# One program block for the attention of both batches, and weights cut ahead of the stage that uses them

## What is computed

```python
t = t + attn(ln(t))      # softmax(q k^T / 16) v over the 4096 tokens of a batch, float32
t = t + lstm(ln(t))      # gates from ln(t) @ U + b, and h @ V step by step over 4096 tokens
```

## Time and profile before

| | us |
|---|---|
| median of 3 runs | 3800.24 |
| lowest, highest | 3799.6, 3802.97 |
| the profiled execution, its time | 3802.11 |
| its span (first to last instruction) | 3800.3 |
| PE busy in it | 3490.2 (92%) |
| DVE, ACT, GpSimd busy | 2919.2, 2443.7, 1313.8 |

### The profile page before, as it was taken

The page is one execution under the profiler, slowest core; times in us unless marked ns, Lnnn a source line. Parts: engine busy times, 40 slices in busy tenths (PEclk is TensorE's granted clock), DMA queues, the critical chain, the costliest instruction groups (busy, mean ns, idle before and its releaser), DMA issues. The chain is left out here.

```text
span 3800.3 us, 81781 instructions
## 1 busy us (share of the span) xinstructions
PE 3490.2 (92%) x30707; PEld 2954.7 (78%) x30707; DVE 2919.2 (77%) x4367; ACT 2443.7 (64%) x6220; POOL 1313.8 (35%) x737
## 2 busy tenths in 40 slices
PE   8878888888889989999999989999999989899987
PEld 7755555555569978888888888888888878888886
DVE  4679999999968866777777766777777766777887
ACT  4548888888855555666666655666666633677775
POOL 0009999999955541000000011000000024222254
PEclk9979999999999989999999999999999989999999
DMA  5674111211124321000000010000000046555575
GB/s 147 197 205 112 44 40 44 61 44 39 44 72 139 114 92 45 18 18 18 18 18 18 18 45 12 18 18 18 18 18 12 12 161 213 167 142 143 146 227 164
DMA packets 198916, 294.19 MB, mean 77 GB/s; under 512 B 17744, under 2 KB 155088, under 8 KB 195536
## 3 DMA queue, kind: packets, MB, share of 16 engines
q1 hardware_dynamic: 189392, 281.88, 24.8%
q10 hardware_dynamic: 9216, 8.39, 0.6%
HBM read 197.67 MB, written 92.54 MB: 76 GB/s over the span
## 5 line engine op out<-in xcount | busy, mean ns | idle before, releaser
L741 POOL TENSOR_TENSOR mx_big<-mp_lvs,mx_big 128x1280 f32<-128x1280 f32 (+1 forms) x224 | 710.1, 3235 | 282.4 <-ACT mp_lvs L661 278.3
L716 DVE TENSOR_TENSOR mx_big<-mp_psL,mx_big 128x2816 f32<-128x2816 f32 (+1 forms) x224 | 691.0, 3142 | 20.7 <-PE mp_psO L606 18.0
L668 ACT ACTIVATE mp_cut<-mp_psO,mx_mask 128x128 f32<-128x128 f32 x2048 | 553.3, 405 | 139.1 <-PE mp_psO L606 109.3
L606 PE MATMUL mp_psO<-mx_big,mp_pair 128*16 128x256 f32 x8192 | 498.5, 383 | 110.0 <-DVE mx_big L716 82.1
L1597 PE MATMUL sv_psO<-at_v_hi,sv_p_hi 128*128 128x258 f32 x2048 | 583.9, 285 | 13.5 <-DVE sv_p_lo L1685 10.4
L1616 ACT ACTIVATE sv_S<-sv_psS,at_kb 128x512 f32<-128x512 f32 x512 | 353.0, 689 | 372.2 <-PE sv_psS L1571 300.2
L1597 PE MATMUL sv_psO<-at_v_lo,sv_p_hi 128*128 128x258 f32 x2048 | 578.7, 283 | 0.0
L1597 PE MATMUL sv_psO<-at_v_hi,sv_p_lo 128*128 128x258 f32 x2048 | 577.9, 282 | 0.0
L1660 DVE TENSOR_TENSOR sv_run<-sv_run,sv_S 128x512 f32<-128x512 f32 x448 | 313.7, 700 | 289.0 <-ACT sv_S L1616 289.0
L606 PEld LDWEIGHTS mp_psO<-mx_big,mp_pair 128*16 128x16 f32 x8192 | 327.6, 126 | 245.3 <-DVE mx_big L716 136.0
L1597 PEld LDWEIGHTS sv_psO<-at_v_hi,sv_p_hi 128*128 128x128 f32 x2048 | 386.3, 189 | 43.1 <-DVE sv_p_lo L1685 21.2
(11 more groups left out here) (301 smaller groups left out, 7723.0 us busy)
## 6 DMA issues: line engine op xcount, KB each, us to landing
re_xg<-xg SPq DMA_DIRECT2D x192, 384.0 KB, 3.3
xg<-ga_xg SPq DMA_DIRECT2D x32, 768.0 KB, 4.0
att<-mx_big SPq DMA_DIRECT2D x16, 1024.0 KB, 6.5
mp_pair<-att SPq DMA_DIRECT2D x128, 128.0 KB, 2.9
mx_big<-rv SPq DMA_DIRECT2D x14, 1024.0 KB, 11.7
fr_xr<-in_x SPq DMA_DIRECT2D x16, 512.0 KB, 4.7
fr_xl<-in_x SPq DMA_DIRECT2D x32, 256.0 KB, 4.2
rv<-fr_rvs SPq DMA_DIRECT2D x16, 512.0 KB, 3.2
```

The lines of the kernel that those rows point to most:

```text
L606: mm = pe.matmul(psO[32 * j:32 * j + 2 * H, c % 2, q, :], pair[:, s, :, :, c * YC + y], Z[:, c % 2, y, :], start=True, stop=True, tile_pos ...
L668: ins = nc.scalar.activation(cut[:, s, c, :, h * DK:(h + 1) * DK], psO[:, c % 2, :, h * DK:(h + 1) * DK], ACT.Copy, scale=mask[:, h:h + 1])
L716: nc.vector.tensor_tensor(Z[:, c % 2, 0:m], psL[:, s, 0:D].unsqueeze(1).broadcast_to([P, m, D]), rv_place(big, seventh, b, c)[:, 0:m], ALU ...
L741: nc.gpsimd.tensor_tensor(Z[:, c % 2, m:YC], lvs[:, s, :].unsqueeze(1).broadcast_to([P, YC - m, D]), rv_place(big, seventh, b, c)[:, m:YC] ...
```

## The change

The four blocks of attention become one. `attention` is split in `projections` and `weighing`, which return one function for each engine; `attention_block` calls them in turn in a single `nc.Block()`. Where a program block's end kept things apart, waits on semaphores now stand. The weights of batch 1 are cut by GpSimd in the last passes of weighing batch 0, its first token blocks are loaded there too, and GpSimd cuts U, the gates' weights, into the space of `k_hi` after the last score of batch 1. The gates' block loads and cuts no weights.

```diff
+def attention_block(nc):
+    with nc.Block() as block:
+        @block.sync
+        def _(sp):
+            clear_used(sp, PLAN["used"])
+            project0.sync(sp)
+            weigh0.sync(sp, project1)
+            project1.sync(sp)
+            weigh1.sync(sp, None)
...
-                clear_used(sp)          # at the end of each attention block
...
     class SecondKeyWeights:
-    def cut_hi(self, act): / def cut_lo(self, dve):
+    def cut(self, pool):
+        pool.wait_ge(self.shared.w_in, 32)
+        self.nc.gpsimd.tensor_copy(self.mt_hi[:, :, :], self.mt).then_inc(self.mt_hi_cut, 1)
+        pool.wait_ge(self.mt_hi_cut, 1)
+        self.nc.gpsimd.tensor_tensor(self.mt_lo[:, :, :], self.mt, self.mt_hi[:, :, :], ALU.subtract).then_inc(self.mt_cut, 1)
...
     projections, tensor:
+                if b > 0 and n == 0:
+                    pe.wait_ge(before.kept, before.units)
+                if b > 0 and n == 1:
+                    pe.wait_ge(before.shifted, before.units)
...
+                if b > 0 and n == 0:
+                    pe.wait_ge(before.evicted, before.evictions)
...
     weighing, sync, after the last loads of batch 0, then of batch 1:
+                    sp.wait_ge(p_kept, NU - R + 9)
+                    after.load_first(sp)                  # token blocks 1 and 2
+                if b > 0 and n == NBLK - 1:
+                    sp.wait_ge(q_cut, BLOCKS - 2)
+                    for j in range(3):
+                        if j == 2:
+                            sp.wait_ge(shared.u_cut, 1)
+                        sp.dma_start(q[:, j % 2, :]..., k_rows(PLAN["gates"][1][j])).then_inc(shared.u_in[j], 16)
...
     weighing, gpsimd:
+            if b == 0:
+                pool.wait_ge(p_kept, NU - R + 5)
+                after.keys.cut(pool)
+            else:
+                pool.wait_ge(scored, NU)
+                for j in range(3):
+                    pool.wait_ge(shared.u_in[j], 16)
+                    nc.gpsimd.tensor_copy(shared.gates_hi[:, :, part], u).then_inc(shared.u_hi_cut, 1)
+                    pool.wait_ge(shared.u_hi_cut, j + 1)
+                    nc.gpsimd.tensor_tensor(shared.gates_lo[:, :, part], u, shared.gates_hi[:, :, part], ALU.subtract).then_inc(shared.u_cut, 1)
...
     weighing, tensor: score(0) waits for k_hi_kept and k_lo_kept of block 6, score(15) of block 7
...
     gates' inputs, sync:
-                sp.dma_start(ident[:, :], ident_d).then_inc(w_in, 16)
-                for j in range(3):
-                    sp.dma_start(w[:, :, j * D:(j + 1) * D], k_rows(u[j])).then_inc(w_in, 16)
     gates' inputs, scalar: keep_hi(0) stands before root(1) now; the three copies of w are gone
     gates' inputs, vector: the three subtractions are gone, and b_in is waited for in round 2, not 0
```

More of the change, by code:

```diff
@@ L52, with clear_used @@
 USED = []
[L55 to L58 removed]
+def clear_used(sp, used=USED):
+    while used:
+        sems, guards = used.pop()
         for sem in sems:
@@ L1343, in attention_phase @@
             dense_layers(nc, early, keys, t_d, xlT_d)
-        PLAN["attention"] = ExitStack()
-        FOLDED["area"] = AttentionArea(nc, PLAN["attention"])
-        attention(nc, b, area, keys, FOLDED["area"], t_d, xlT_d, wvT, t2_d)
-    else:
[L1348 to L1353, removed]
+        PLAN["used"] = USED[:]
@@ new lines, in attention_phase @@
+        USED.clear()
+        PLAN["base"], PLAN["top"] = ExitStack(), ExitStack()
+        shared = FOLDED["area"] = AttentionArea(nc, PLAN["base"], PLAN["top"])
+        first = projections(nc, b, area, keys, shared, xlT_d)
+        PLAN["first"] = first, weighing(nc, b, first, shared, t_d, xlT_d, wvT, t2_d)
+    else:
+        shared = FOLDED["area"]
+        keys = SecondKeyWeights(nc, area, shared)
+        third = projections(nc, b, area, keys, shared, xlT_d)
+        fourth = weighing(nc, b, third, shared, t_d, xlT_d, wvT, t2_d)
+        PLAN["last"] = third, fourth
@@ L1355, in attention, with projections @@
+Projections = collections.namedtuple("Projections", "sync tensor scalar gpsimd vector load_first keys k_hi_kept k_lo_kept v_lo_kept v_biased kb_made")
+Weighing = collections.namedtuple("Weighing", "sync tensor scalar gpsimd vector kept shifted p_kept evicted units evictions")
+def projections(nc, b, area, keys, shared, xlT_d):
     NT = T // P
@@ new lines, in load_first, with weighing @@
+        def load_first(sp):
+            for n in (1, 2):
+                keys.load_tokens(sp, xlT_d, b * T, n)
+    return Projections(sync=sync, tensor=tensor, scalar=scalar, gpsimd=gpsimd, vector=vector, load_first=load_first, keys=keys,
+                    k_hi_kept=k_hi_kept, k_lo_kept=k_lo_kept, v_lo_kept=v_lo_kept, v_biased=v_biased, kb_made=kb_made)
+def weighing(nc, b, made, shared, t_d, xlT_d, wvT, t2_d):
+    BLK = 512
+    NBLK = T // BLK
+    KB = BLK // P
+    VW = D + 2
+    ident, k_hi, k_lo, v_hi, v_lo, q_hi, q_lo, kb, q, t, t2_out = (
+        shared.ident, shared.k_hi, shared.k_lo, shared.v_hi, shared.v_lo, shared.q_hi, shared.q_lo, shared.kb, shared.q, shared.t, shared.t2_out)
@@ new lines, in scalar, with keep, exponent, keep_hi @@
+        def scalar(act, after):
+            def keep(u):
+                if u == 0:
+                    act.wait_ge(made.kb_made, NBLK * 2)
+                if u == SC:
+                    act.wait_ge(made.v_lo_kept, NBLK * 2)
+                act.wait_ge(scored, u + 1)
+                reach(act, p_kept, u - R + 1)
+                nc.scalar.activation(S[:, u % R, :], psS[:, u % 2, :], ACT.Identity, bias=kb[:, u % C:u % C + 1]).then_inc(kept, 1)
+            def exponent(u):
+                act.wait_ge(shifted, u + 1)
+                nc.scalar.activation(S[:, u % R, :], S[:, u % R, :], ACT.Exp, scale=SCALE).then_inc(exped, 1)
+            def keep_hi(u):
+                act.wait_ge(exped, u + 1)
+                reach(act, weighed, u - 1)
+                nc.scalar.copy(p_hi[:, u % 2], S[:, u % R, :]).then_inc(hi_kept, 1)
+            def evict(m):
+                act.wait_ge(weighed, (m + 1) * SC)
+                reach(act, added, m // 2 * KB)
+                for j in range(KB):
+                    nc.scalar.copy(acc[:, j, :], psO[:, j, 0:VW]).then_inc(evicted, 1)
+                act.wait_ge(differed, m // 2 + 1)
+                nc.scalar.activation(fade[:, :], fall[:, :], ACT.Exp, scale=SCALE).then_inc(faded, 1)
+            for u in range(NU + LAG + 1):
+                done = u - 1 - LAG
+                if done >= 0 and done % C == SC - 1:
+                    evict(done // SC)
+                if u < NU:
+                    keep(u)
+                if 0 <= u - SC < NU:
+                    exponent(u - SC)
+                    keep_hi(u - SC)
@@ L1718 @@
+    return Weighing(sync=sync, tensor=tensor, scalar=scalar, gpsimd=gpsimd, vector=vector,
+                    kept=kept, shifted=shifted, p_kept=p_kept, evicted=evicted, units=NU, evictions=2 * NBLK * KB)
 class RecurrentWeights:
```

588 lines of the change are left out of this document (292 added, 296 removed).

## The result

The changed kernel's median is 3778.87 us (3777.17 to 3783.27, 5 runs); the kernel before has 3800.24 (3799.6 to 3802.97, 5 runs). The ratio is 0.9944, 95% interval 0.993 to 0.9957: 21.4 us less, where 17.5 were predicted. The profiled execution took 3778.66 us, its span is 3776.8. That sum is 2380.74 us before and 2359.37 after: 21.37 less.

The account below looks back on a forecast made before the run. PE, busy 3490.2 of 3800.3 us, was taken as the bound, so gains lie in its holes and low clock. Terms -10.2 - 8.0 - 4.8 + 3.0 + 2.2 + 0.25 = -17.5 took the median 3800.24 to 3782.7 us, range 3777 to 3790.

Parts of the forecast that it names:

- joint, batch 0 and 1: Projections to weighing, twice: PE goes straight on, 3.5 us of hole and 1.6 of lower clock saved, 5.1 us each.
- middle: Weighing of batch 0 to projections of batch 1: DVE cuts block 1 right after its last finish sum, 8.0 us gained.
- GpSimd's cuts: Last 18 units of weighing: five subtractions each hold a p_lo for half their length, 3.0 us lost, bounds 0.8 and 8.8.
- 18 clears ahead of the gates: Before the gates' block: SP no longer clears 18 semaphores at 0.063 us each, 1.1 us gained.
- first products: Start of the gates' block: keep_hi(0) follows turn(0) at once, so the first gate products come 3.7 us sooner.
- 85 clears behind them: End of the gates' block: SP clears 85 semaphores after its last store, delaying the recurrence by 2.2 us, bounds 1.5 and 3.
- the rest of the end: Last blocks: seven semaphores more and three fewer to clear, 0.25 us lost.
- tile period, first raw copy: Gates' block after the first products: tiles bound by PE as before, everything behind keeps its distance, so no gain counted.
- GpSimd at 8.8: Rival in the last units of weighing: GpSimd holds DVE much longer, 8.8 us instead of 3.0, giving 3788.5 us; chance 0.12.
- the products not earlier: Rival in the gates' block: bias or second tile sets the first products, 3.7 us goes, 3786.4 remains; chance 0.08.
- PE's own supply: Rival at projections to weighing: PE's instruction supply makes the holes, so they stay and 10.2 us is lost, 3792.9; chance 0.08.
- Another round: Rival in the recurrence: U's changed rounding makes again ask for one more round, some 180 us, about 3960; chance 0.03.

Follow-up runs that it names:

- the split kernel: The changed kernel with its one block cut into three, where each projection gives way to its weighing; median 3790.71 us, ratio 0.9968 to the kernel before.
- The split: The changed kernel with its block cut in two between weighing of batch 0 and projections of batch 1, tokens and weights still loaded ahead; 3784.99 us.
- the kernel with U late: The changed kernel with GpSimd's parting of U held back until 13 units before the end of batch 1's weighing; 3785.08 us.

## Why the prediction was right, and where its sizes were off

The direction, the places that were named and the range held. The terms, predicted and measured in the sums:

| | predicted | measured |
|---|---|---|
| joint, batch 0 and 1 | -5.1, -5.1 | -5.15, -5.08 |
| middle | -8.0 | -8.07 |
| GpSimd's cuts | +3.0 | +0.95 +0.10 |
| 18 clears ahead of the gates | -1.1 | -0.91 |
| first products | -3.7 | -3.73 |
| 85 clears behind them | +2.2 | +1.89 |
| the rest of the end | +0.25 | +0.56 |
| tile period, first raw copy | 0 | -1.29, -0.88 |

The tile period's term is taken from GpSimd's first bias addition to its last. What is left, +0.24, is 0.13 between the gates' first load and turn(0), and 0.11 spread over the projections and the passes.

- **Joints.** Right in both parts, the hole and the clock; the block end is the cause, since it brings both back. What the low clock costs after such a hole is less sure than the prediction had it: 1.5 to 1.6 in both places of before against after, 1.73 and 2.95 in the split kernel.
- **Middle.** Size right. The prediction gave the loop over DVE as what decides, and its start as the gain. The split shows that PE's late first block counts too: DVE started only 1.96 later there, the loop 4.8.
- **GpSimd's cuts: the mis-sized term.** The step "one meets each subtraction and waits on average half of it" failed. DVE waits only if GpSimd started first. Six cuts among the last units held up one `p_lo` in batch 0, and six held up one in the kernel with U late; of the other ten, six started just behind a DVE subtraction or ran into one and waited themselves, four met none. The Trainium skill has this too, in SBUF — State Buffer, section "Who interferes with whom": the order of issue, not the operation, decides who blocks. The rows agree: 0.07 behind cost 0.99, 0.04 ahead cost nothing. And U's cuts fell into the end of a pass, where PE stands anyway. The lower bound of 0.8, from the pass ends, was the better row; the price of 4 us that the prediction laid over the timeline by the page's rule was too high, though the rule itself held, since it doesn't say who will start first.
- **Gates.** 3.7 right. The tile period was held for bound by PE "as before"; it shortened from 4.65 to 4.61. From the first bias addition to the last the 32 tiles took 145.36 us before and with the gates' block of before, 143.14 to 144.50 in all traces with U's halves in `k_hi`. Of the 1.29 some 1.1 are the period (31 steps of 0.034); the rest is a single step, the fifth, which varies from 4.61 to 5.52 among the traces with U's halves in `k_hi`. The raw copy's 0.88 is the clock's and lies within the spread of one kernel: that part of the gain is luck.
- **Clears.** 0.060 us each for 0.063, if the prediction's 0.3 of entry holds: (5.73 - 0.36) less 0.3 over 85. The 18 ahead of the gates gave 0.91, 0.05 each. The 56 at the start are hidden as predicted: from the store of `mt` to the last value matmul of batch 0 it takes 52.8 us before and 52.3 to 53.0 in the traces of the changed kernels. The 0.25 for the last blocks can't be told from noise: from the recurrence's first load to the end it takes 565.3 us before and 565.4 to 566.8 in the others.
- **Rivals.** GpSimd at 8.8, the products not earlier, and PE's own supply are each excluded by a row above. Another round didn't come: 192 loads of `re_xg` in all kernels.

The 3.9 us more than predicted are thus 2.0 of contention that didn't come, 1.3 of tiles, 0.9 of spread and 0.3 of the 85 clears, less 0.6 in the other terms. The first is a size that was wrong, the second was not foreseen, and the third is chance.

## What to carry to other kernels

A block end costs the wait for the slowest engine, here 3.5 us of PE, and then 1.5 to 3 us lost at half clock; where only semaphore waits take its place, both go; here the timeline of before gave the gain of each joint to a tenth of a us. Put work for GpSimd where the chain pauses anyway, or give it to engines that have a gap at the right moment (0.95 us here), and clear semaphores beside a loop instead of between two stages (1.9). Compare stretches between marks behind the last unchanged instruction: an edit of 3 us is lost in medians when the part ahead varies by nine.

## What was not expected of the hardware

The part of the program ahead of the attention ended 9.5 us apart in thirteen traces (1414.17 to 1423.70), while the 659 us of the passes of batch 0 agreed within 0.3 in all of them. The products of a gate tile took 4.65 us with U's halves in tensors of their own and 4.60 to 4.61 with them in `k_hi`, the code being the same otherwise. In the kernel split at the joints PE was back at its full pace of 0.23 us per score matmul 4.0 us after one hole of 3.8 us and 6.4 us after the other, with its matmuls dense in both.
